# Attention and FFN layer: the rows of the Q and K stacks put in another order

## The reference

```
Q = split_heads(x)                       # 16 channels per head
K = split_heads(x @ Wk + bk)
V = split_heads(x @ Wv + bv)             # 64 channels per head
o = softmax(Q K^T + causal mask) V
a = x + gelu(o) @ Wf + bf
y = layernorm(x + a)
out = layernorm(y + ffn(y))              # silu(y wg) * (y wu), then wd; int8 weights, 768 hidden
```

## Time and profile before

| | us |
|---|---|
| median of 3 runs | 2096.61 |
| lowest and highest | 2093.05, 2106.03 |
| the profiled execution | 2108.82 |
| its span, first to last instruction | 2107.1 |
| PE busy in the span | 1911.4 (91%) |
| DVE busy | 1523.5 (72%) |
| POOL busy | 1125.3 (53%) |
| ACT busy | 1036.1 (49%) |
| share of the 16 DMA engines, queue of SP | 46.6% |

### The profile page before, as it was taken

The page is one execution under the profiler, slowest core; times in us unless marked ns, Lnnn a source line. Parts: engine busy times, 40 slices in busy tenths (PEclk is TensorE's granted clock), DMA queues, the critical chain, the costliest instruction groups (busy, mean ns, idle before and its releaser), DMA issues. The chain is left out here.

```text
span 2107.1 us, 38558 instructions
## 1 busy us (share of the span) xinstructions
PE 1911.4 (91%) x10304; PEld 980.5 (47%) x10304; DVE 1523.5 (72%) x3598; ACT 1036.1 (49%) x1523; POOL 1125.3 (53%) x1192
## 2 busy tenths in 40 slices
PE   6699999999999999999999999878879899989996
PEld 4344444344444444444444444323256675757664
DVE  3687878778787777877777787767337676767764
ACT  2155555555555555555554555434535454545543
POOL 0067677676776767767767767566702122221212
PEclk9599999999999999999999999878889999999998
DMA  8535445354453544535444454541054655556440
GB/s 286 179 127 171 167 129 173 116 177 159 132 170 125 176 158 132 168 123 174 147 150 155 131 167 122 182 118 60 22 141 138 163 156 143 163 136 176 123 110 21
DMA packets 257711, 303.59 MB, mean 144 GB/s; under 512 B 24736, under 2 KB 174368, under 8 KB 257584
## 3 DMA queue, kind: packets, MB, share of 16 engines
q1 hardware_dynamic: 244784, 300.13, 46.6%
q10 hardware_dynamic: 12800, 2.11, 0.6%
HBM read 174.20 MB, written 127.93 MB: 143 GB/s over the span
## 5 line engine op out<-in xcount | busy, mean ns | idle before, releaser
L915 ACT ACTIVATE weights<-ring 128x1024 f32<-128x1024 f32 (+3 forms) x768 | 596.2, 810 | 359.4 <-PE ring L662 335.2
L632 POOL TENSOR_TENSOR weight_sum<-weight_sum,weights 128x512 f32<-128x512 f32 (+3 forms) x448 | 680.1, 1518 | 9.6
L662 PE MATMUL o_acc<-weights,v_pair 128*64 128x512 f32 (+3 forms) x3072 | 635.1, 519 | 28.9 <-ACT weights L915 10.3
L610 POOL TENSOR_SCALAR_AFFINE_SELECT weights<-weights 128x256 f32<-128x256 f32 x512 | 220.0, 434 | 400.8 <-ACT weights L915 394.1
L1086 DVE TENSOR_REDUCE part_max<-ring 128x2 f32<-128x1024 f32 x256 | 300.3, 1215 | 129.7 <-PE ring L662 129.5
L662 PE MATMUL ring<-q_stack,k_stack 50*128 50x512 f32 (+3 forms) x1536 | 315.5, 417 | 47.7 <-DVE rowmax L1094 25.1
L653 POOL TENSOR_TENSOR h_lo<-hidden,h_hi 128x512 f16<-128x512 f32 x96 | 114.2, 1190 | 450.1 <-ACT h_hi L883 450.1
L662 PE MATMUL ring<-k_stack,q_stack 48*128 48x512 f32 (+3 forms) x1536 | 310.6, 407 | 42.5 <-DMA k_stack<-k_rows 25.9
L1094 DVE CUSTOM_DVE_ANT_0 scrap<-ring,causal 128x128 bf16<-128x128 f32 (+3 forms) x512 | 229.5, 485 | 114.7 <-PE ring L662 113.2
L662 PEld LDWEIGHTS o_acc<-weights,v_pair 128*64 128x64 f32 x3072 | 175.6, 139 | 265.0 <-issue 227.9
L1094 DVE CUSTOM_DVE_ANT_0 scrap<-ring,causal,part_max 128x128 bf16<-128x128 f32 (+3 forms) x512 | 251.2, 547 | 39.6 <-PE ring L662 36.2
(11 more groups left out here) (105 smaller groups left out, 2165.1 us busy)
## 6 DMA issues: line engine op xcount, KB each, us to landing
v_pairs<-v_unit SPq DMA_DIRECT2D x64, 512.0 KB, 12.4
v_pair<-v_pairs SPq DMA_DIRECT2D x64, 512.0 KB, 12.8
o_heads<-o_pair SPq DMA_DIRECT2D x64, 512.0 KB, 5.2
g<-o_heads SPq DMA_DIRECT2D x16, 2048.0 KB, 8.2
den_wide<-reciprocals SPq DMA_DIRECT2D x32, 1024.0 KB, 16.0
q_stack<-q_rows SPq DMA_DIRECT2D x128, 192.0 KB
k_stack<-k_rows SPq DMA_DIRECT2D x128, 192.0 KB
q_rows<-x_hi SPq DMA_DIRECT2D x32, 512.0 KB, 5.2
```

Of the source, the lines that this page charges most:

```text
L610: pool.affine_select(out=diag, in_=diag, compare_op=ALU.is_ge, fill=0.0, base=0, pattern=[[0, 2], [1, P]], channel_multiplier=-1).then_inc ...
L632: pool.tensor_tensor(dst, other, W[t][:, :, :], ALU.add).then_inc(s_add, 1)
L662: return nc.tensor.matmul(o, l, r, start=start, stop=stop)
L915: nc.scalar.activation(W[t][:, :, :], bank_of("t", t)[:, :, 0:width_of(t)], ACT.Exp).then_inc(s_w, 1)
```

## The change

Only the source pattern of the four stack loads is another. Before, the walk over HBM goes part by part and inside a part channel by channel, so partition 16 * m + d holds part m of channel d. Now it goes channel by channel with the three parts inside, so partition 3 * d + m holds part m of channel d. It is the same for Q and K. The source pattern goes from (3 parts, 16 channels, 1024) to (16 channels, 3 parts, 1024); the destination is 48 partitions of 1024 floats in both. The bytes, the 4 KB rows and the number of DMAs stay; so do all instructions of all engines and their order.

```diff
@@ -410,7 +410,7 @@
                     for h in range(2):
                         sp.dma_start(stack[slot][HSTEP * h:HSTEP * h + SROWS, :].bitcast(F32),
                                      rows.rearrange("m b h d t -> m (b h) d t")[:, bass.ds(2 * n + h, 1)].rearrange(
-                                         "m o d t -> m (o d) t")).then_inc(s_stack[slot], 16)
+                                         "m o d t -> (o d) m t")).then_inc(s_stack[slot], 16)
```

## The result

| | median us | lowest to highest | runs |
|---|---|---|---|
| before | 2100.18 | 2093.05 to 2107.49 | 20 |
| the change | 2111.71 | 2098.01 to 2122.02 | 20 |

The ratio is 1.0045, 95% interval 1.0027 to 1.0063. So it is slower beyond its noise by some 10 us, within the 1% taken as "no change". The profiled execution of the change took 2107.93 us (span 2106.2), among the shorter ones. That of the kernel before took 2108.82 us, more than any of its 20 above. So the two profiles can't be compared as a whole, only stretch by stretch, and where a stretch carries an argument the profiles of the experiments stand beside it.

The account below looks back on a forecast made before the run. PE was taken to bound the middle of stage B, with stack loads hidden there. Gains of 9 us at the start and 6 near the end made 15 us, to 2081.6 us against the median of 2096.61; range 2070 to 2096.

Parts of the forecast that it names:

- How a stack load is dealt out: Stack loads: a DMA is dealt by its outermost dimension, three engines before, all 16 with the new pattern.
- The start, forecast 9: Start of stage B: first stacks land sooner and PE starts 9 us earlier, bounds 4.6 to 9.4, passed on in full.
- The end, forecast 6: Near the end of stage B: PE's 7.9 us wait on a stack load mostly goes, gaining 6 us.
- SP's issues, forecast 0: SP's 256 stack DMA issues, about 0.78 us each, keep their time: 0, bounds 0.4 us per DMA either way.
- PE, DVE, POOL and ACT have the same instructions in the same order: 0: Whole kernel: these four engines' instructions and order are unchanged, so they were priced at 0.
- in this stretch a faster stack load is worth nothing: Middle of stage B: stack loads go out a pair ahead and land unseen under PE work, gain 0.
- The ACT wait, 0: 100 to 1300 us: ACT's four waits on shift stores, 7.5 us in all, priced 0 given 40 us slack in 88.
- rival D: All pairs: shift stores land up to 1.9 us later behind stack rows, delaying ACT and PE; 2118 us, 5%.
- A: Stack loads: the dealing does not change, three engines as before, 2096.6 us; chance 10%.
- B: Stack loads: rows 8 MiB apart come slower, 7.6 us in place of 10.1, giving 2091.6 us; chance 8%.
- C: Last pairs and start: clock of last pairs comes back and ramp runs faster, 25 us gain, 2071.6 us; chance 22%.
- a faster ramp: 63 to 100 us: PE leaves the low clock sooner, ramp a tenth faster, 4 us more.

Follow-up runs that it names:

- experiment 4: The change with SP's three K stores moved behind the stores of o and of the denominators, against the kernel before: 2071.96 us, ratio 0.9860.
- experiment 7: The kernel before, old source pattern, with the three K stores issued ahead of the next pair's stack loads: 2164.27 us, ratio 1.0292.
- experiment 8: The change with the three parts of q_rows and k_rows one 4 KB row further apart in HBM, against the kernel before: ratio 1.0046.
- its control: The kernel before, old source pattern, with the three K stores moved behind the stores of o and of the denominators: 2102.97 us, ratio 1.0009.

## Why the prediction was wrong, by its steps

- **How a stack load is dealt out:** right. A share of 0.19 meant three engines, and the new pattern takes more: a wait of 8.2 us in place of 18.0, and stacks that land in 3.6 to 4.2 us. The Trainium skill's rule on the number of engines (DMA: Bandwidth & Descriptors, "Why a DMA increments its semaphore by 16 and not by 1") gave 16. The runs agree with it: the share is 1.10 in the window from 50 to 55 us, and each stack load has 13 small packets more, 16 less 3.
- **The start, forecast 9:** 8.7 from the first issue to the first matmul. Right. The first pair comes 10.6 us sooner in the two profiles, but 1.9 of these are chance. **The end, forecast 6:** 7.6 over the last twelve pairs. Right in direction and rather low: in the profiles with the new pattern at the end these pairs take 271 to 276 us, in those with the old one 282 to 287, so the gain is nearer to 10.
- **SP's issues, forecast 0:** the duration was about right. The four stack issues at the start took 2.56 us in place of 3.11. What failed is what they do to the queue behind. The prediction saw it at the start, where it read 12.53 us of V stores as full queues, and did not ask what the same backlog does in each unit of the middle. There a K store stood 7.14 us, and so 1.5 MB were kept away from ACT's issue.
- **"PE, DVE, POOL and ACT have the same instructions in the same order: 0":** this is the step that failed. The instructions are the same, their meeting with the DMA queue is not. In the middle it cost 16.6 us over forty pairs and 3.7 in the first eleven. With the K stores late the same forty pairs gained 12.7, which makes the step 29 us off there. That gain is missed too: "in this stretch a faster stack load is worth nothing" looked only at PE's wait for the stacks.
- **The ACT wait, 0, and rival D at 5%:** D had the right four instructions and the wrong half of them. It priced their landing behind the stack rows as up to 1.9 us later. The last of them landed about 1 us sooner, and ACT's 7.5 us in four waits are gone from the list. That D's 2118 us lie near the 2111.71 measured is chance. The prediction took ACT's own queue and slack as protection. It was their issue that grew, by 1.8 us in one pair of four. ACT's slack of 40 us in 88 did not help, as the work behind it is what PE waits for at that moment. The stack rows had no part in it (experiments 4 and 7).
- **Rivals A, B and C:** A is out by the start wait, B by experiment 8. C had more gain in the last pairs than the sum, and experiment 4 has 11.7 us in the last twelve. PE's granted clock over them is 0.89 before, 0.90 with the change and 0.91 there, and of the 11.7 us 6.7 are less busy time and 5.0 less idle time; so the clock has a part, of unknown size. Its other half, a faster ramp, did not come: from pair 0 to 11 are 231.1 us in experiment 4 and 230.0 in its control.

**Open:** how much of the 12.7 us of the middle in experiment 4 is the earlier landing of the shifts. The gain is in the third and fourth pair of a unit (means over the forty 22.2 and 24.6 us before, 21.7 and 24.0 there), and 5.3 us of it stand in PE's busy time, at an unchanged clock of 1.00. Open too is by what means three queued stores lengthen an issue on another engine's queue; the runs show only that three do and one does not, and one unit with two and a third just beginning that was as slow as with three.

## What to carry to other kernels

A slow transfer can act as a gate: before you speed one up, list what is queued behind it on the issuing engine, when that will go out instead, and which engine issues small, urgent DMAs at that moment. An engine's slack does not protect it if what stands behind the delayed instruction is what the bound engine waits for next. A wait that a trace puts at a few us can hide a landing that is late nearly every time; ask what becomes of it when the engines are freed. And a "no change" can be a gain and a loss: here 0.6% won at the ends and 1.05% lost in the middle, and a reordering of one SP line that is worth nothing by itself turned it into 1.4%.

## What the runs showed of the hardware

- A DMA whose source pattern begins with 3 against 48 partitions ran at 78 GB/s on a share of 0.19; beginning with 16, the same 786 KB were in place 5.95 us after the first of four issues, issue time included. Each such DMA had 13 more packets under 512 B.
- The issue of four 4 KB stores on ACT's queue took 1.81 us even at a DMA share of 1.12, and 3.4 to 3.9 us when SP had queued three stores of 512 KB in the 2 us before; with one such store 1.8 to 2.1 us.
- The last of these four landed about 1 us later beside stack loads on three engines (share 0.19 for a load alone) than beside loads on all of them: 4.6 to 5.0 against 3.5 to 3.8 us from the end of the issues to the next step of ACT.
- An SP issue can itself stand 7 us behind loads of the old pattern. In the list of DMAs this shows only as a longer duration (7.14 against 0.39 us), and in no list of waits.
- A PE gap of 1.99 us in a dense stretch was followed by clock 0.50 from 611 to 615 us.
